# Expert outputs are added to one DRAM row per token by the scatter; the final sum of two rows goes, and VectorE takes two copies at the square roots

## The reference

```python
xn = layernorm(x)
s  = differential_attention(xn, wq, wk, wv, wo)     # 8 heads, causal, RMS norm over groups of 4
logits = xn @ router_weight.T + router_bias         # 8 experts
top_w = softmax(top_k(logits, 2))                   # two experts for each token
gate, up = xn @ gate_up_proj[e] + bias[e]           # 256 -> 2 x 256, even and odd columns
glu = min(gate, 7) * sigmoid(1.702 * min(gate, 7))
y_e = ((clip(up, -7, 7) + 1) * glu) @ down_proj[e] + down_bias[e]
out = x + s * silu(sum over the token's two experts of top_w * y_e)
```

## Time and profile before

| | us |
|---|---|
| median of 3 runs | 1004.12 (1003.0 to 1006.98) |
| profiled execution, device time | 1007.79 |
| its span, first to last instruction | 1006.1 |
| PE busy in the span | 907.2 (90%) |
| DVE busy | 883.6 (88%) |
| ACT busy | 768.9 (76%) |
| POOL busy | 285.1 (28%) |

### The profile page before, as it was taken

How to read it: one execution, slowest core, us unless ns; L and a number is a source line. 1 busy time by engine, 2 the same in 40 slices (tenths; PEclk the granted TensorE clock), 3 DMA queues, 4 the chain that set the end, 5 groups by cost and what they waited for, 6 DMA issues and landing times.

```text
span 1006.1 us, 24046 instructions
## 1 busy us (share of the span) xinstructions
PE 907.2 (90%) x6642; PEld 644.2 (64%) x6642; DVE 883.6 (88%) x1759; ACT 768.9 (76%) x2012; POOL 285.1 (28%) x486
## 2 busy tenths in 40 slices
PE   8999975889989899999989989998889999999987
PEld 6877763666666666666666666666656666656676
DVE  6687866999999999999999999999948888868848
ACT  4554434999999999999999999999945555564453
POOL 2000001323332332333201010000236666656610
PEclk9999995999999999999999999999999999999999
DMA  7989975485666758666576645546013333332369
GB/s 241 337 316 316 292 265 159 98 202 134 145 156 167 151 129 193 142 139 162 111 141 89 147 100 126 124 104 146 13 32 111 106 111 123 113 100 86 102 202 323
DMA packets 89456, 157.27 MB, mean 156 GB/s; under 512 B 19548, under 2 KB 48732, under 8 KB 89372
## 3 DMA queue, kind: packets, MB, share of 16 engines
q1 hardware_dynamic: 80544, 137.56, 52.4%
q0 software_dynamic: 8864, 19.15, 6.1%
HBM read 104.30 MB, written 52.36 MB: 156 GB/s over the span
## 4 chain that ended last, share of the span: by engine, by line
PE 30%; DVE 23%; ACT 15%; issue 13%; ACTq 1%; DMA 1%; DVEq 0%; SPq 0%; POOL 0%; POOLq 0%
PE bank L1029 12%; DVE Pr_long L1784 7%; DVE nmax L1734 7%; PE bank L1055 6%; ACT Pr_long L1655 5%; PE bank L1537 5%; ACT Pr_short L1669 5%; DVE nmax L1752 5%; ACT AT L1682 4%; PE bank L1578 2%; PE bank L1015 1%; PE bank L1042 1%; PE bank L1539 1%; DVE nmax L1746 1%; DVE coef L1771 1%
## 5 line engine op out<-in xcount | busy, mean ns | idle before, releaser
L1734 DVE TENSOR_REDUCE nmax<-bank 128x1 f32<-128x1024 f32 (+3 forms) x256 | 260.1, 1016 | 6.6 <-PE bank L1539 6.6
L1655 ACT ACTIVATE Pr_long<-bank,nmax 128x1024 f32<-128x1024 f32 (+3 forms) x256 | 252.6, 987 | 10.7 <-DVE nmax L1734 10.5
L1682 ACT COPY AT<-bank 128x512 f32<-128x512 f32 (+3 forms) x384 | 177.5, 495 | 3.9 <-PE bank L1578 2.1
L1537 PE MATMUL bank<-Ks_first,Qs_first 128*128 128x512 f32 (+3 forms) x384 | 123.4, 411 | 28.2 <-ACT Pr_short L1669 17.2
L1404 POOL COPY VO<-Ob 128x64 f32 (+1 forms) x128 | 30.2, 236 | 417.0 <-ACT Ob L1691 415.2
L1669 ACT ACTIVATE Pr_short<-bank,nmax 128x128 f32<-128x128 f32 (+3 forms) x256 | 138.7, 542 | 9.7 <-DVE nmax L1752 2.3
L1578 PE MATMUL bank<-ident,Pr_long 128*128 128x128 f32 x832 | 127.7, 280 | 18.4 <-DVE Pr_long L1784 18.3
L1029 PE MATMUL bank<-gu_sb,xsT 128*128 x284 | 136.1, 602 | 4.8 <-ACT xsT L1123 4.0
L1537 PE MATMUL bank<-Ks_second,Qs_second 128*128 128x512 f32 (+3 forms) x384 | 119.3, 399 | 20.7 <-ACT Pr_short L1669 20.6
L1784 DVE SCALAR_TENSOR_TENSOR Pr_long<-Pr_long,coef 128x1024 f32<-128x1024 f32 (+3 forms) x128 | 137.6, 1075 | 0.0
L1539 PE MATMUL bank<-maskb,identb 128*128 128x128 bf16 x512 | 117.7, 233 | 0.0
(11 more groups left out here) (170 smaller groups left out, 1612.0 us busy)
## 6 DMA issues: line engine op xcount, KB each, us to landing
q_parts<-PARTS SPq DMA_DIRECT2D x32, 512.0 KB, 3.4
k_parts<-PARTS SPq DMA_DIRECT2D x32, 512.0 KB, 3.9
Qs_first<-q_parts SPq DMA_DIRECT2D x64, 256.0 KB
Ks_first<-k_parts SPq DMA_DIRECT2D x64, 256.0 KB
Qs_second<-q_parts SPq DMA_DIRECT2D x64, 256.0 KB
Ks_second<-k_parts SPq DMA_DIRECT2D x64, 256.0 KB
X<-x SPq DMA_DIRECT2D x8, 512.0 KB, 5.3
xn_dram<-XN SPq DMA_DIRECT2D x8, 512.0 KB, 6.5
```

What stands on the lines that cost most here:

```text
L1537: nc.tensor.matmul(at[:, c0:c1], Qs[head][:, m, q * P:(q + 1) * P], Ks[head][:, m, c0:c1], start=True, stop=(c1 < N))
L1655: nc.scalar.activation(long_probs(p)[:, m, 0:N], long_slot[m][:, 0:N], ACT.Exp, bias=nmax[:, 4 * p + m:4 * p + m + 1], scale=1.0, accum_ou ...
L1682: nc.scalar.copy(AT[u % 6][:, 0:w], tb[u % BANKS][:, 0:w]).then_inc(unit_out, 1)
L1734: nc.vector.tensor_reduce(nmax[:, 4 * p + m:4 * p + m + 1], long_slot[m][:, 0:N], AX.X, ALU.max, negate=True).then_inc(long_maxed, 1)
```

## The change

- `y_dram` has one row per token (and 256 spare rows for empty slots). The scatter adds to the row (`compute_op=ALU.add`). Two results of one token are in different tiles, so scatter n waits on POOL until scatter n-1 has landed.
- The T rows are zeroed by four SP transfers of 1 MB, behind the head loads of attention iterations 8 and 9. The SP loop over these two iterations is unrolled.
- The closing part loads 8 transfers in place of 16, and DVE's `sum_experts` goes; ACT's silu waits on the load itself.
- The gate's curve is silu(1.702 v) in place of the sigmoid form of gelu; the factor 1/1.702 moves into ACT's copy in `act_out`. With one table for the gate and the closing silu, the load at L1206 goes.
- At the end of attention ACT copies the first two turned tiles ahead of the table load, not behind it and two more copies.
- In step 51 (`ROOT_TILE + 1`) DVE does `rows_out` of tile 53 and `act_out` of tile 51 in ACT's place.

```diff
-Y_ROWS = TOP_K * T + ROW_BUFS * P
+Y_ROWS = T + ROW_BUFS * P
...
                     def results_out(n):
                         pool.wait_ge(y_weighted, n + 1)
-                        pool.indirect_dma_start(y_dram, bass.IndirectOffsetOnAxis(slots[:, n, 1:2], 0),
-                                                ys[n % ROW_BUFS][:], None).then_inc(y_stored[n % ROW_BUFS], 16)
+                        if n == 0:
+                            pool.wait_ge(y_zeroed, 16 * 4)
+                        else:
+                            pool.wait_ge(y_stored[(n - 1) % ROW_BUFS], 16 * ((n - 1) // ROW_BUFS + 1))
+                        pool.indirect_dma_start(y_dram, bass.IndirectOffsetOnAxis(slot_out[:, n:n + 1], 0),
+                                                ys[n % ROW_BUFS][:], None, compute_op=ALU.add
+                                                ).then_inc(y_stored[n % ROW_BUFS], 16)
...
                     for c in range(NCH):
-                        for k in range(TOP_K):
-                            sp.dma_start(yg[c][:, :, k, :], y_v[k, c]).then_inc(y_loaded[c], 16)
+                        sp.dma_start(yg[c][:, :, 0, :], y_v[c]).then_inc(y_loaded[c], 16)
...
-                    nc.scalar.activation(glu[u][:], hid[u][:, 0:I], GLU).then_inc(glu_ready, 1)
+                    nc.scalar.activation(glu[u][:], hid[u][:, 0:I], ACT.Silu, scale=ALPHA).then_inc(glu_ready, 1)
...
-                    nc.scalar.activation(silu_table[:], ident[:, 0:1], ACT.Silu)
...
+                        if m == ROOT_TILE + 1:
+                            dve.wait_ge(xsT_ready, seen(0, m + 1))
+                            rows_copied(m + 2)
                         output(it, n - 1, e)
-                        norms(2 * it + n)
+                        norms(m)
+                        if m == ROOT_TILE + 1:
+                            dve.wait_ge(act_T_ready, seen(0, m - 1))
+                            act_copied(m)
...
-                    def sum_experts(c):
-                        dve.wait_ge(y_loaded[c], 16 * TOP_K)
-                        nc.vector.tensor_tensor(yg[c][:, :, 0, :], yg[c][:, :, 0, :], yg[c][:, :, 1, :], ALU.add
-                                                ).then_inc(ff_ready, 1)
...
+                    def zero_rows(z):
+                        sp.dma_start(y_z[z], zeros[:].unsqueeze(1).broadcast_to([P, ZERO_TILES, D])).then_inc(y_zeroed, 16)
...
-                    with sp.Fori(E, SORT_ITS + 2) as it:
+                    for it in range(E, SORT_ITS + 2):
                         for u in range(2):
                             load(it + 1, u)
+                            zero_rows(2 * (it - E) + u)
```

More of the change, by code:

```diff
@@ L14 @@
 AX = mybir.AxisListType
-GLU = ACT.Gelu_apprx_sigmoid
+ALPHA = 1.702
 B, S, D = 4, 1024, 256
@@ L185, in build @@
         slot_tokens = sb("slot_tokens", [P, SLOT_TILES], I32)
+        slot_out = sb("slot_out", [P, SLOT_TILES], I32)
+        zeros = sb("zeros", [P, D])
         xs = [sb(f"xs{u}", [P, D]) for u in range(ROW_BUFS)]
@@ L233, in build @@
         consts_done = sem("consts_done")
+        zeros_ready = sem("zeros_ready")
+        y_zeroed = sem("y_zeroed")
         lam_step = sem("lam_step")
@@ L1143, in act_out @@
                     nc.scalar.wait_ge(y_bank, seen(it, u - 2))
-                    nc.scalar.copy(act_T[u][:].rearrange("p c n -> p (c n)"), abank[u][:, 0:HC * P]
-                                   ).then_inc(act_T_ready, 1)
+                    nc.scalar.mul(act_T[u][:].rearrange("p c n -> p (c n)"), abank[u][:, 0:HC * P], 1.0 / ALPHA
+                                  ).then_inc(act_T_ready, 1)
                 def first_rows_out(act):
@@ L1180, in step @@
                     def step(it, n, e):
-                        rows_out(it, n + 2)
+                        m = 2 * it + n
+                        if m == ROOT_TILE + 2:
+                            act.wait_ge(xsT_ready, seen(0, m + 1))
+                            act.wait_ge(act_T_ready, seen(0, m - 1))
+                        if m != ROOT_TILE + 1:
+                            rows_out(it, n + 2)
                         gate_curve(it, n + 1)
-                        act_out(it, n)
+                        if m != ROOT_TILE + 1:
+                            act_out(it, n)
                         weigh(it, n - 1)
-                        squares(2 * it + n)
-                        if 2 * it + n == ROOT_TILE:
+                        squares(m)
+                        if m == ROOT_TILE:
                             roots()
@@ L1305, in norms, with rows_copied, act_copied @@
                             nc.vector.reciprocal(rest, rest).then_inc(inverted, 1)
+                    def rows_copied(m):
+                        u = m % 2
+                        dve.wait_ge(xs_turned, seen(0, m))
+                        dve.wait_ge(hid_bank, seen(0, m - 2))
+                        nc.vector.tensor_copy(xsT[u][:].rearrange("p c n -> p (c n)"), xbank[u][:, 0:HC * P]
+                                              ).then_inc(xsT_ready, 1)
+                    def act_copied(m):
+                        u = m % 2
+                        dve.wait_ge(act_turned, seen(0, m))
+                        dve.wait_ge(y_bank, seen(0, m - 2))
+                        nc.vector.tensor_scalar(act_T[u][:].rearrange("p c n -> p (c n)"), abank[u][:, 0:HC * P],
+                                                1.0 / ALPHA, None, ALU.mult).then_inc(act_T_ready, 1)
                     def step(it, n, e):
+                        m = 2 * it + n
                         activate(it, n)
@@ L1484, in tokens_of_slots @@
                         pool.wait_ge(rows_known, 16)
-                        for i, (row, token) in enumerate(((slot_rows, slot_tokens[:]), (slot_tokens[:], slot_tokens[:]))):
+                        for i, (row, token) in enumerate(((slot_rows, slot_out[:]), (slot_out[:], slot_tokens[:]))):
                             past = xs_first[:, 0:SLOT_TILES].bitcast(I32)
@@ L1714, in behind @@
                         if p == NP - 3:
-                            nc.scalar.activation(gate_table[:], ident[:, 0:1], GLU)
-                        if p == NP - 2:
                             first_rows_out(act)
+                            nc.scalar.activation(gate_table[:], ident[:, 0:1], ACT.Silu)
                     run_pairs(act, 4, frame, behind)
```

13 lines of the change are left out of this document (6 added, 7 removed).

## The result

The changed kernel takes 1128.8 us (median of 6 runs, 1126.57 to 1131.55), the kernel before 1005.31 us in the same comparison: ratio 1.124, 95% interval 1.1221 to 1.1259. It is 12% slower. The prediction said slower, but with 1037, at most 1100; the loss is nearly four times the one forecast. The profiled execution took 1131.55 us, with a span of 1129.8 us.

What follows compares the result with a forecast made beforehand. PE was taken to bound the third stage at 3.02 us a tile, the scatter chain then setting 3.6 us: +38.6 - 2.6 - 1.7 - 1.5 = +32.8 us, median 1036.9 (predicted 1037), range 997 to 1100.

Steps and rivals of the forecast that it cites:

- e = 0.7, L = 3.3, and a turn of 3.6 us: Third stage's scatter chain: adding costs e = 0.7 us, landing time L becomes 3.3, each turn 3.6 us; +38.6 us.
- 69 L - 194.9: Whole kernel's change in us as a function of scatter landing time L; zero at L = 2.82.
- The upper bound, a serial read of 1.55 us: Scatter's landing: adding repeats the part behind the issue once more; as a rival +91 us, 1095, chance 0.20.
- the signs of being wrong: Adding issue much longer than 1.05 us, granted clock falling with PE's pauses, gathers too late, or landings under 2.8 us.
- So 0.3: POOL's start of the next scatter behind a landing, put at 0.3 us from a 0.27 us start behind ACT's multiplication.
- So 2.6 for the mean: Plain scatter's mean landing time from issue start, put at 2.6 us; median 2.5, worst 3.8.
- the fitting rival: Third stage: with adding cost below about 0.15 us, turns stay under 3.02 and PE paces; -5.7 us, 998.4, chance 0.26.
- The end of the stage: Third stage into closing part: PE starts 3.4 us ahead of the last scatter, 2.6 us earlier against it; -2.6 us.
- The closing part: DVE's sums go and its last multiplication starts when PE's last bank is done; -1.7 us.
- The end of attention: ACT's copies ahead of the table load let PE's first gate and up product start earlier; -1.5 us.
- The roots: Square roots in the third stage: 1.5 of 4.1 us lost stay; -2.5 us where PE sets the pace.
- The gather ... I cost at nothing: POOL's gather of tile n+5 runs late behind scatter n-1, but its rows are used two turns later; no cost.

Runs made afterwards that it cites:

- experiment 2: The changed kernel with a plain scatter that overwrites instead of adding, the wait on the last landing kept: 1032.47 us, ratio 1.0271.
- experiment 4: The changed kernel with POOL's two waits ahead of the scatter swapped, the landing first and ACT's rows last: 1085.62 us, ratio 1.08.
- experiment 6: The changed kernel with swapped waits, adding only 128 of 256 columns into a tensor with rows of 512 bytes: 1051.2 us, ratio 1.0454.
- experiment 7: The changed kernel with four buffers of result rows in place of two: 1123.24 us, ratio 1.1176.
- experiment 5: The changed kernel with both a plain scatter that doesn't add and POOL's two waits swapped: 1008.07 us, ratio 1.0033.
- experiment 1: The kernel before with silu, early copies at attention's end and DVE's copies at the roots; scatters, loads and closing sums unchanged: 1001.68 us, ratio 0.9971.
- experiment 10: The changed kernel with plain scatters and swapped waits, its eight loads of x issued together at the third stage's start: 1012.69 us, ratio 1.0064.
- experiment 11: The changed kernel with DVE's normalisation multiplication (L1289) cut to a few columns: 1124.87 us, ratio 1.1168.
- experiment 8: The kernel before with silu, early copies and DVE's root copies, plus three of DVE's eight closing sums moved to POOL: 1002.49 us, ratio 0.997.

## Why the prediction was wrong

**The mechanism was right.** That the landing of a scatter decides, that the chain takes over the pace from PE, that DVE and POOL then wait for landings, and that none of the small gains can pay for it: all in the traces, and experiments 2, 4, 6 and 7 bear it out. The step that failed is the size of the turn: "e = 0.7, L = 3.3, and a turn of 3.6 us". It measured 4.55 undisturbed and 4.89 in the mean. Put into the sum's own form, 69 L - 194.9 with a mean L of 4.12 (4.89 less the restart of 0.77) gives +89; the missing 0.47 us of restart for 70 turns gives +33; together 1004.1 + 122 = 1126. The form of the sum held; three of its terms didn't.

**First term: what adding adds.** 1.40 us a turn (experiment 2), where I took 0.7 for lying "nearer to the bytes than to the serial read". That is 0.7 x 70 = 49 us of the miss. The upper bound, a serial read of 1.55 us, was near in size only: 0.6 of the 1.40 us is a longer issue, which I had left at 1.05 us in every case but the last; it took 1.59 (0.98 in experiment 2). That was one of the signs of being wrong that the prediction named. The queue row shows another form of transfer: 15680 packets for 19.15 MB, where the kernel before had 8864 for as many bytes:

```profile
q0 software_dynamic: 8864, 19.15, 6.1%
```

So they are smaller; that this is the cause of the longer issue was not tried. The Trainium skill's rule (page "DMA: Bandwidth & Descriptors", section on the anatomy of a GpSimd DMA) is about 2 us fixed plus the bytes over 436 GB/s, by which doubling the bytes adds an estimated 0.3 us. For the plain scatter it is near (2.3 us by the rule, 2.4 measured in experiment 5); for the adding one it is not, since experiment 2 gives 1.40 us: an adding scatter is not a plain one with twice the bytes.

**Second term: the restart.** "So 0.3" was read from a scatter that waited on ACT alone. In the changed kernel it stands behind two waits, and the one that is fulfilled last, written second, is an instruction of its own ahead of the scatter. It cost 0.77 us, 0.80 in the mean: 0.5 x 70 = 35 us of the miss. In the swapped order it was 0.28 (experiment 4), and the time fell by 43 us, 34 of them the restart itself and the rest shorter landings.

**Third term: the mean.** "So 2.6 for the mean": plain landings had a median of 2.5 with some of 3.8, and I let 0.1 us stand for those. In the chain of experiment 2 their mean was 2.70, another 0.1 x 70 = 7 us of the miss. The three terms, 49 + 35 + 7, make up the 90 us by which 70 turns of 4.89 us exceed 70 of 3.6; the whole difference between forecast and result is 91.8, and the smaller terms below run both ways. In a chain each long landing is lost in full: even with plain writes and the restart as I had put it, the kernel was slower than before and not 5.7 us faster (experiment 5). So the fitting rival, to which I gave 0.26, would not have come out at 998.4 even for e = 0.

**What else can be set against its steps.** PE's clock: in the stage 0.96, near to what was said; but in the last tiles it fell to 0.50 and stayed there until 1092.7, and three instructions of the closing part took 0.88 + 0.88 + 1.61 = 3.4 us more. The end of the stage: PE begins 4.55 us ahead of the last scatter and not 3.4. The closing part: from PE's start to DVE's end 41.4 us (39.5 before), less 3.4 for the clock, so -1.5 where -1.7 was said; DVE ends 2.3 us behind PE, said 1.9. The end of attention: -1.6 to -1.75 for PE, said -1.5; the -3.0 of the first scatter is within what executions differ by. The roots: two table loads, as said, and -2.5 only where PE paces (experiment 1). Zeroing: at nothing, as said; its transfers took 11.0 us each to land, and attention didn't grow. "The gather ... I cost at nothing": PE waits 77 us for gathers, but they are late because POOL is, and when DVE's wait was taken away the time fell by only 5.6 us (experiment 7).

**What stays open:** whether the instruction packets of experiment 10 are what lengthens the landings that no load of x explains (342.0 less 70 x 4.55 are 23.5 us lost to disturbed turns, of which 6 are the long issues of experiment 11 and some 7 the eight loads of x; the five landings beside such a packet alone are together 7 us over 3.85), why half of them do no harm, and how the part of the flight that doesn't go with the bytes divides between read and write.

## What to carry to other kernels

When a change puts a landing into a cycle, price the cycle by its mean and not by the median of a landing, and add each part of it separately: issue, flight, and the restart of the engine that waits; an error of 0.1 us in one is 7 us after 70 turns. Where an instruction has two waits, see in the trace which of them is a sequencer's row of its own, and let it be the one that is fulfilled early; here that was the one written second, so the late one belongs first. Where bounds for an unknown cost are a factor of three apart and the sum hangs on it alone, measure the operation by itself before the kernel is rewritten around it: here the rows written twice and summed at the end were far cheaper than rows added in memory, and the best version is the one that keeps them and takes only the small rearrangements (experiment 1, ratio 0.9971).

## What the runs showed of the hardware

- An indirect scatter of 128 rows of 1 KB takes 1.59 us to issue when it adds, 0.98 to 1.05 when it writes; with rows of 512 bytes still 1.59. It lands 3.8 to 3.9 us after the issue's start in the median, against 2.4; with 512 bytes 3.4.
- Of two waits ahead of a scatter, the one written second was an instruction of its own. When it was the late one the scatter started 0.77 us after the landing; when the late one rode on the scatter, 0.28 us (experiment 4).
- A DVE multiplication of 128 x 512 with two operands in SBUF beside a scatter's issue lengthened it from 1.60 to 1.93 us (experiment 11). A POOL sum of 128 x 1024 beside a DVE addition of that size lengthened the addition from 1.23 to 2.37 us; a DVE multiplication with one operand in PSUM kept its time beside it (experiment 8).
- Pauses of PE in each turn (244 of 340 us busy) left the granted clock at 0.96 in the mean. It fell to 0.50 (1.2 GHz) at 1075.7, after 6 us in which PE was busy for 1.81, and PE's instructions then took 2.07 for 1.12 us, 1.97 for 1.09 and 5.23 for 3.62.
- One load of 512 KB beside an adding scatter lengthened its landing from 3.8 us to between 4.6 and 5.0 (experiment 4). In the changed kernel the landings of 4.6 to 5.8 us without such a load all had a packet of 16 KB on an instruction queue in flight; that it is the cause was not tried.
